# Gate transposition moved behind a projection, a key norm root moved ahead of two silus, mask products added ahead of waits, and a feed-forward loop in another order

## The reference

```python
# layer 0, mixer: a delta rule over the 37 tokens, 16 heads of 16
states = scan(rotate(state) + (x @ cond_in_W))            # 128 wide
deltas = rmsnorm(states) @ delta_W                        # q, k, v and gate parts
q, k, v = silu(causal_conv4(x @ ctrl_W + ctrl_b + deltas))
q, k = l2norm(q), l2norm(k)
S = g*S;  S = S + k (x) (beta * (v - k S));  o = q S      # 37 steps per head
x = x + (rmsnorm(o) * silu(gate)) @ out_proj_W.T
# layer 0, feed-forward: quantized, 1024 hidden
y = silu(conv3(bit_linear(act_quant(layernorm(x)), w1)));  x = x + bit_linear(act_quant(y), w2)
# layer 1: softmax attention with 16 heads, then a mixture of 32 experts
# (8 of 32 by a grouped router, and shared experts), weights streamed from HBM
```

## Time and profile before

| what | value |
|---|---|
| median of 3 runs | 898.96 us (898.91 to 900.83) |
| profiled execution | 899.29 us, span 897.6 us |
| PE / PEld busy | 762.5 us (85%) / 562.6 us (63%) |
| DVE / ACT / POOL busy | 614.6 us (68%) / 389.3 us (43%) / 185.9 us (21%) |
| mean granted clock of PE | 0.933 |
| chain that ended last | PE 70%, DVE 18%, ACT 5%, issue 4% |

### The profile page before, as it was taken

One profiled execution on the slowest core, in us unless ns is written; L12 is line 12 of the kernel. 1 busy time (PEld: TensorE's weight loads), 2 busy tenths in 40 slices (PEclk: granted clock), 3 DMA queues, 4 the chain that ended last, 5 costly groups with the idle time before them and its releaser, 6 DMA issues.

```text
span 897.6 us, 19046 instructions
## 1 busy us (share of the span) xinstructions
PE 762.5 (85%) x7314; PEld 562.6 (63%) x7314; DVE 614.6 (68%) x974; ACT 389.3 (43%) x559; POOL 185.9 (21%) x197
## 2 busy tenths in 40 slices
PE   4786956989996966877598996699999999999997
PEld 3554735954543654656278884467777777777775
DVE  5796597658877476788767887757777755555554
ACT  5344653620224232765356983434444423333322
POOL 7000791005989801000300430000000000000000
PEclk9986877999999996987999998889999999999999
DMA  8000000020000000010112001044444312222221
GB/s 304 1 1 2 2 1 3 3 95 0 1 0 1 0 2 0 1 33 6 35 30 59 14 28 36 1 148 147 157 151 151 125 53 79 65 68 62 67 65 54
DMA packets 24070, 46.02 MB, mean 51 GB/s; under 512 B 2605, under 2 KB 10541, under 8 KB 23629
## 3 DMA queue, kind: packets, MB, share of 16 engines
q1 hardware_dynamic: 24013, 45.21, 16.5%
HBM read 41.91 MB, written 1.36 MB: 48 GB/s over the span
## 4 chain that ended last, share of the span: by engine, by line
PE 70%; DVE 18%; ACT 5%; issue 4%; POOL 1%; DMA 1%; SPq 0%; DVEq 0%; ACTq 0%; POOLq 0%
PE psum L1765 11%; PE psum L1766 11%; PE psum L1767 11%; PE psum L1941 6%; PE psum L1951 4%; PE psum L825 4%; PE psum L826 4%; PE psum L827 4%; PE psum L2069 1%; DVE arena L1445 1%; PE psum L1991 1%; PE psum L1922 1%; DVE arena L1638 1%; DVE arena L1310 1%; PE psum L2108 1%
## 5 line engine op out<-in xcount | busy, mean ns | idle before, releaser
L1765 PE MATMUL psum<-xh,arena 128*128 128x296 f16 (+1 forms) x664 | 196.4, 296 | 12.0 <-DVE xl L1318 6.3
L1766 PE MATMUL psum<-xl,arena 128*128 128x296 f16 (+1 forms) x664 | 196.3, 296 | 0.0
L1767 PE MATMUL psum<-xh,arena 128*128 128x296 f16 (+1 forms) x664 | 196.1, 295 | 0.0
L694 DVE TENSOR_TENSOR arena<-arena 128x592 f16<-128x592 f32 x68 | 52.7, 776 | 61.2 <-ACT arena L605 60.9
L600 ACT ACTIVATE arena<-psum 128x592 f32<-128x592 f32 x66 | 43.8, 664 | 115.3 <-PE psum L1767 115.3
L1765 PEld LDWEIGHTS psum<-xh,arena 128*128 (+2 forms) x664 | 66.2, 100 | 35.6 <-issue 9.4
L749 DVE TENSOR_TENSOR arena<-psum,arena 128x592 f32<-128x592 f32 x64 | 49.6, 775 | 50.9 <-PE psum L1767 50.2
L825 PE MATMUL psum<-arena 128*128 128x296 f16 x272 | 79.7, 293 | 4.6 <-DVE arena L694 3.8
L826 PE MATMUL psum<-arena 128*128 128x296 f16 x272 | 79.7, 293 | 0.0
L605 ACT ACTIVATE arena<-arena 128x592 f16<-128x592 f32 x66 | 46.0, 697 | 77.6 <-DVE arena L688 74.8
L827 PE MATMUL psum<-arena 128*128 128x296 f16 x272 | 79.6, 293 | 0.0
(11 more groups left out here) (317 smaller groups left out, 1583.1 us busy)
## 6 DMA issues: line engine op xcount, KB each, us to landing
arena<-comb SPq DMA_DIRECT2D x62, 296.0 KB, 3.3
arena<-in_wmoe SPq DMA_DIRECT2D x34, 384.0 KB, 3.0
arena<-in_xt SPq DMA_DIRECT2D x4, 864.0 KB, 9.5
arena<-in_w SPq DMA_DIRECT2D x2, 1024.0 KB, 6.6
arena<-arena SPq DMA_DIRECT2D x6, 187.0 KB
arena<-in_ctrl SPq DMA_DIRECT2D x1, 1056.0 KB, 9.1
out<-arena SPq DMA_DIRECT2D x2, 512.0 KB, 3.1
arena<-in_wlin SPq DMA_DIRECT2D x1, 768.0 KB, 4.4
```

Source lines behind the costliest of these rows:

```text
L694: dve.tensor_tensor(al[:, s_], t1, ah[:, s_], ALU.subtract).then_inc(ev["al"], 1)
L1765: pe.matmul(dst, wh, mh, start=start, stop=False)
L1766: pe.matmul(dst, wh, ml, start=False, stop=False)
L1767: return pe.matmul(dst, wl, mh, start=False, stop=stop)
```

## The change

Five things are changed.

1. `dbT` stands behind all four qkv(1, q), on PE, on ACT (its sigmoid) and in the plan of the banks.
2. ACT takes the root of `n2` right behind the evacuation of qkv(5), ahead of silu(4) and silu(5); DVE takes the reciprocal before the two `low_v` steps, and the second of them stands behind the first quarter of `n2r`.
3. `keep_clock(ps, n)` puts n products of the mask with the identity (128 x 296, bf16) into a bank that the next result will overwrite, ahead of a wait of PE. The numbers are in the table `KEEP`; the rec entry is used five times (four layer norms and `cr`), split three times, tok twice, the others once: 5 x 16 + 3 x 12 + 2 x 12 + 18 + 12 + 20 + 12 + 12 + 14 + 36 + 32 + 30 + 24 = 350 products. Where `fill` stood behind a wait it now stands ahead of it.
4. `AT` is made by a plain f32 product with the identity in place of a transposition, and only of the columns from s0 on.
5. In the feed-forward loop `fab` has 4 slots, the absolute values of a pair are taken one iteration later and in the order odd, even, the running maximum stands between the evacuation of `f1` and the convolution (LARGEST is its order), and the last four maxima are taken at the end. Row 0 is scaled on DVE straight out of PSUM, in three pieces, before ACT copies the factors to SBUF (`mx2_read`).

```diff
--- before.py
+++ after.py
@@ -122,9 +122,9 @@
         for q in range(NCH):
-            if m == 1 and q == 2:
-                add(("dbT",), "act")
             add(("qkv", m, q), "act")
+        if m == 1:
+            add(("dbT",), "act")
     add(("n2",), "act")
@@ -200,9 +200,12 @@
 ROUNDED = (0, 2, 4, 6)
+LARGEST = (1, 0, 3, 2, 5, 4, 7, 6)
 HIGH_AT = [7, 9, 11, 13]
...
 FILLERS = 4
+KEEP = {"rec": 16, "mx1": 18, "tok": 12, "xq": 12, "mx2": 20, "hq": 12, "split": 12, "combine": 12, "op": 14, "csq": 36,
+        "qkrec": 32, "km": 30, "on": 24}
 VT = (B + 2) // 3
@@ -428,7 +431,7 @@
         ft = carve(5120, 2, T)
-        fab = carve(33964, 2, T)
+        fab = carve(33964, 4, T)
@@ -852,6 +855,8 @@
                 if hf == 0:
+                    after(pe, ("ln4", "m", 1))
+                    keep_clock(banks[GATE_UP], KEEP["split"])
                     pe.wait_ge(ev["ln4_xl"], 2)
@@ -1113,7 +1118,7 @@
                                        bias=sm("dbb", rows=slice(0, 32))).then_inc(ev["dbh"], 1)
-            for q in range(2):
+            for q in range(NCH):
                 projected(1, q)
@@ -1126,16 +1131,16 @@
                     return
+                act.activation(vh[:, m - 4], post[:, m], ACT.Copy).then_inc(ev["vh"], 1)
+
+            for m in range(1, 6):
+                if m >= 2:
+                    act.wait_ge(ev["conv"], m - 1)
+                for q in range(NCH if m == 1 else 0, NCH):
+                    projected(m, q)
                 if m == 5:
...
                     act.activation(nrm, bank(("n2",))[:, 0:CH], ACT.Sqrt, bias=eps[:, 1:2]).then_inc(emptied["act"], 1)
-                act.activation(vh[:, m - 4], post[:, m], ACT.Copy).then_inc(ev["vh"], 1)
-
-            for m in range(1, 6):
-                if m >= 2:
-                    act.wait_ge(ev["conv"], m - 1)
-                for q in range(2 if m == 1 else 0, NCH):
-                    projected(m, q)
                 through_silu(m - 1)
@@ -1211,17 +1216,29 @@
                         full(act, (name, kind, n))
+                        if (name, kind) == ("mx2", "r"):
+                            act.wait_ge(ev["mx2_read"], n + 1)
                         act.activation(dst[:, 512 * n:512 * n + w], bank((name, kind, n))[:, 0:w], ACT.Copy).then_inc(emptied["act"], 1)
...
             act.activation(warm[:, 1:2], eps[:, 0:1], ACT.Silu)
+            def magnitudes(f):
+                act.wait_ge(ev["sil"], f // 2 + 1)
+                after(act, ("fc", f + 1, NCH - 1))
+                for x in (f + 1, f):
+                    if f >= 4:
+                        act.wait_ge(ev["am2"], LARGEST.index(x - 4) + 1)
+                    act.activation(fab[:, x % 4], sil[:, x], ACT.Abs).then_inc(ev["fabs"], 1)
+
             for f in range(0, FC, 2):
...
                                         bias=sm("fcb", f)).then_inc(ev["fy"], 1)
+                if f:
+                    magnitudes(f - 2)
                 for q in range(NCH):
@@ -1229,19 +1246,17 @@
                 act.activation(sil[:, f], fy, ACT.Silu).then_inc(ev["sil"], 1)
-                act.wait_ge(ev["sil"], f // 2 + 1)
-                after(act, ("fc", f + 1, NCH - 1))
-                for x in (f, f + 1):
-                    if f:
-                        act.wait_ge(ev["am2"], x - 1)
-                    act.activation(fab[:, x % 2], sil[:, x], ACT.Abs).then_inc(ev["fabs"], 1)
+            magnitudes(FC - 2)
             act.wait_ge(ev["l_wqkv"], 16)
...
             for i, f in enumerate(ROUNDED):
-                act.wait_ge(ev["scaled"], i + 1)
+                if i:
+                    act.wait_ge(ev["scaled"], i)
+                else:
+                    act.wait_ge(ev["mx2_read"], 3)
                 link(act.activation(sil[:, f], sil[:, f], ACT.Identity, bias=eps[:, 2:3]))
@@ -1453,12 +1468,13 @@
                         low_db(3)
-            for m in range(2):
+            def low_v(m):
                 dve.wait_ge(ev["vh"], m + 1)
                 dve.tensor_tensor(vl[:, m], post[:, 4 + m], vh[:, m], ALU.subtract).then_inc(ev["vl"], 1)
-                if m == 0:
-                    after(dve, ("n2",))
-                    dve.reciprocal(nrm, nrm).then_inc(ev["qkrec"], 1)
+
+            after(dve, ("n2",))
+            dve.reciprocal(nrm, nrm).then_inc(ev["qkrec"], 1)
+            low_v(0)
@@ -1474,6 +1490,8 @@
                     low_qk(m - 1)
+                else:
+                    low_v(1)
             low_qk(3)
@@ -1632,11 +1650,12 @@
-            def largest(f):
-
-                dve.wait_ge(ev["fabs"], f + 1)
-                dve.tensor_tensor(am, fab[:, 0] if f == 0 else am, fab[:, f % 2], ALU.max).then_inc(ev["am2"], 1)
-                dve.wait_ge(ev["am2"], f + 1)
+            def largest(i):
+                dve.wait_ge(ev["fabs"], i + 1)
+                if i:
+                    dve.wait_ge(ev["am2"], i)
+                now = fab[:, LARGEST[i] % 4]
+                dve.tensor_tensor(am, am if i else now, now, ALU.max).then_inc(ev["am2"], 1)
@@ -1649,24 +1668,30 @@
                                                  wsum[:, 2:3], mxb[:, cols(q)], ALU.mult, ALU.mult).then_inc(emptied["dve"], 1)
+                if f >= 4:
+                    largest(f - 4)
+                    largest(f - 3)
                 dve.wait_ge(ev["fy"], f // 2 + 1)
...
                                                   y[:, :, 0:S - 1], ALU.mult, ALU.add).then_inc(ev["fconv"], 1)
-                if f:
-                    largest(f - 2)
-                    largest(f - 1)
-            largest(FC - 2)
-            largest(FC - 1)
+            for i in range(FC - 4, FC):
+                largest(i)
             token_max("mx2")
...
             dve.tensor_tensor(gwl, gwr, gwh, ALU.subtract).then_inc(ev["gwl"], 1)
+            for n in range(3):
+                t = slice(512 * n, min(512 * n + 512, T))
+                full(dve, ("mx2", "r", n))
+                dve.tensor_tensor(sil[:, 0, t], sil[:, 0, t], bank(("mx2", "r", n))[:, 0:t.stop - t.start], ALU.mult).then_inc(
+                    ev["mx2_read"], 1)
+            dve.wait_ge(ev["mx2_read"], 3)
             after(dve, ("mx2", "r", 2))
-            for f in range(FC):
+            for f in range(1, FC):
                 if f in ROUNDED:
@@ -1766,6 +1791,11 @@
+            def keep_clock(ps, n):
+                for _ in range(n):
+                    pe.matmul(ps[:, 0:8 * S], identb, causalb.unsqueeze(1).to_broadcast([128, 8, S]), start=True,
+                              stop=True)
+
             def norm(name, source, lead=None):
@@ -1785,6 +1815,9 @@
                 ins.then_inc(filled[who((name, "v"))], 1)
+                if name == "ln1":
+                    pe.wait_ge(ev["masks"], 1)
+                keep_clock(fill((name, "r", 0)), KEEP["rec"])
                 pe.wait_ge(ev[name + "_rec"], 1)
@@ -1807,8 +1840,10 @@
             def condition(i, q):
+                ps = fill(("p", i, q))[:, 0:CH]
+                if (i, q) == (0, 0):
+                    keep_clock(ps, KEEP["split"])
                 pe.wait_ge(ev["ln1_xl"], q + 1)
-                ps = fill(("p", i, q))[:, 0:CH]
                 for k in range(2):
@@ -1850,9 +1885,12 @@
             for q in range(NCH):
+                if q == 2:
+                    keep_clock(fill(("cr", 0)), KEEP["csq"])
                 pe.wait_ge(ev["csq"], q // 2 + 1)
...
             ins.then_inc(filled[who(("cv",))], 1)
+            keep_clock(fill(("cr", 0)), KEEP["rec"])
             pe.wait_ge(ev["crec"], 1)
@@ -1867,17 +1905,17 @@
                 for q in range(NCH):
-                    if m == 1 and q == 2:
-                        after(pe, ("db", NCH - 1))
-                        ps = fill(("dbT",))
-                        for t in range(S):
-                            for hg in range(HG):
-                                dst = ps[32 * hg:32 * hg + 32, 8 * t:8 * t + 8]
-                                pick = identh[0:32, 0:32].rearrange("p (i x) -> p i x", i=2)[:, :, 4 * hg:4 * hg + 4]
-                                pe.matmul(dst, seq(dbh)[:, :, t], pick, start=True, stop=False)
-                                ins = pe.matmul(dst, seq(dbl)[:, :, t], pick, start=False, stop=True)
-                        ins.then_inc(filled[who(("dbT",))], 1)
                     projection(m, q)
+                if m == 1:
+                    after(pe, ("db", NCH - 1))
+                    ps = fill(("dbT",))
...
+                    ins.then_inc(filled[who(("dbT",))], 1)
@@ -1887,6 +1925,7 @@
             ins.then_inc(filled[who(("n2",))], 1)
+            keep_clock(fill(("n2r", 0, 0)), KEEP["qkrec"])
             pe.wait_ge(ev["qkrec"], 1)
@@ -1907,6 +1946,8 @@
                     _, j, c, n_ = key
+                    if (j, c, n_) == (0, 0, 0):
+                        keep_clock(ps, KEEP["km"])
                     pe.wait_ge(ev["km"], 2 * j + c + 1)
@@ -1919,7 +1960,10 @@
                     for x in range(ns):
```

(39 more changed lines are left out.)

16 lines of the change are left out of this document (12 added, 4 removed).

## The result

| | median | lowest to highest | profiled execution |
|---|---|---|---|
| before | 899.89 us (4 runs) | 898.91 to 901.34 | 899.29 us, clock 0.933 |
| after | 957.28 us (4 runs) | 944.18 to 963.64 | 963.64 us, clock 0.898 |

The ratio is 1.0529, with an interval of [1.0457, 1.0601]; it compares the two runs of 944.18 and 951.06 alone, because those of 963.50 and 963.64 count as slow ones by their time, while the median of all four is 6.4% above that of before. The forecast was 901.0 with a range from 885 to 912. The runs after are spread over 19.5 us, which the kernel before never showed.

A forecast was written before the change was run, and what follows sets the result against it. The prediction saw two kinds of time to win, PE's waits at seams between stages and its half-clock work, with the A stage PE-bound. Gains against +22.9 for AT, +1.4 and +0.8 summed to +1.75: 901.0 us, range 885 to 912.

The forecast's parts named there:

- I add 1.4 for the last groups, of 7 and 1 times: A stage: allowance on top of +22.9 for AT's loads; a lost clock, up to 5 us more, was the upper end.
- The fourth rival: A stage loses its clock in AT as in dbT, 0.50 for 10 to 20 us: +5 to +10, 908 us; chance 0.07.
- The third convolution: Front: earlier dbT and warmer products let it begin at 97.4 in place of 103.75, 6.3 us won, bounds 5.0 and 7.2.
- what was taken for the root: Key norm: reciprocal ends 3.0 us sooner, against a second table load of 1.28; 1.8 us won, bounds 0 and 3.0.
- the warm A stage: Start of the A stage: part of 3.89 us at half clock saved by warmth, 1.3 us won, at most 1.9.
- The gate transposition's move: Front: the changed order of dbT by itself, counted as 1.0 us won.
- Output norm and ln2 to `xq`: Output norm net 0.4 us won; ln2 and mx1, with warmer broadcast and sums, 1.6 won, bounds 0 and 2.5.
- The loop, mx2 and ln3: Feed-forward loop 4.3 us won by moving absolute values and maxima, mx2 1.9, third layer norm 1.3.
- ln4 and combine with what follows: Fourth layer norm 2.75 us won by warmer products; combine and the products behind it 1.7, bounds 0 and 4.4.
- The first (the seams give more): Won terms at their upper bounds, clock held at nearly every seam: 891 us, or 895 two thirds there; chance 0.22.
- the second (cheap `AT`): A stage: plain products pipeline at the transposition's pace or better, +9.6 and below; 887 or 876 us; chance 0.13.
- The third (the products don't hold the clock): At the seams, added products run out before waits end: 918 us, or 910 with half the warmth; chance 0.2.

The follow-up runs named there:

- the cut version alone: The kernel before with only AT changed, to plain f32 products of the columns from s0 on; 959.45 us, ratio 1.0649.
- the moves alone: The changed kernel with AT transposed again and all KEEP numbers at 0; 895.43 to 897.35 us (three runs) and 919.88 to 922.05 (four).
- the transposed version: The changed kernel with AT made by the 148 transpositions again; 905.24 us, ratio 1.004.
- the experiment: The changed kernel with AT transposed, no added products at the third layer norm, and feed-forward loop and row 0 as before; 885.98 us.

## Why the prediction was wrong

**The step that failed** is the sentence "I add 1.4 for the last groups, of 7 and 1 times", with its bound "up to 5 us more". The clock cost 35.2 there: the stage grew by 58.1, of which 22.9 was forecast for the loads. The pace of a load was right to 2%, 0.112 for 0.11. The fourth rival named the mechanism (the f32 pairs at 0.50, as in `dbT`) and had a chance of 0.07 and 5 to 10 us; it took the loss for a spell that ends by itself. In the trace it ended only behind the stage (at 0.50 from 162.5 to 244 us), and in the cut version alone it did the same (88.0 us). The earlier trace rows showed PE at 0.50 while it was busy, and showed it for a stretch of 8 columns a product; the step should have priced the whole stage at half clock as its bound. From the prediction's own numbers the upper bound was not 5 but some 56 us: 23.8 of A products (33.4 less 9.6) and 32.5 of `AT`, each taking twice as long. The prediction's own sign, some 62 us from the first A product to the end of `AT`, came out at 97.5.

**The second step that failed** was not in the sum at all: every stage not touched was taken over at its time of before. The attention lost 23.4 us in the profiled execution. With 23.4 here, 35.2 there, and the forecast's +1.75 less its 1.4, the sum would be 899.3 + 0.35 + 58.6 = 958.2. The 5.4 that are missing to the profiled 963.6 are gains that came out smaller than forecast (below). What brings the second loss on stays open: the runs show that it comes with the added products alone (78.1 us for the stage) as well as with the moves alone (in 4 of 7 runs), and that 17 products in its pauses prevent it but for one short fall.

**The terms one by one.** The third convolution began at 98.08, forecast 97.4 (before 103.75): 5.7 of 6.3 won. From the chain of waits of the changed kernel:

```profile
98.08 0.85 DVE arena L1454
...
117.16 1.37 DVE arena L1460
118.54 1.91 DVE arena L1476
120.45 1.01 DVE arena L1473
...
121.62 1.57 DVE arena L1488 x4
```

The reciprocal (L1476) now follows the last convolution (L1460) at once, as forecast, and the root's load is off the chain. It began 8.8 us earlier than before, 5.7 of these from the front, so 3.1 for the root. But `AT` began only 7.5 earlier (8.1 in the transposed version): what was taken for the root (1.8) and the warm A stage (1.3) came to 1.8 to 2.4 behind the 5.7, and not 3.1. The gate transposition's move, put at about 1, is nothing that can be measured.

Output norm and ln2 to `xq`: 1.4 with the change, forecast 2.0. The loop, mx2 and ln3: 7.5 forecast, 5.9 measured. Of these the loop itself gave 4.0 against the kernel before (30.9 us from the first to the last `f1`, then 27.0) and 5.0 in the experiment, forecast 4.3; mx2 and ln3 gave 2.0, forecast 3.2. ln4 and combine with what follows: 2.2, forecast 4.45. In sum 17.1 won, forecast 22.55 (23.35 less 0.8). The sizes were some 30% too high in sum, and no group was wrong in sign.

**The rivals.** The first (the seams give more) and the second (cheap `AT`) did not happen. The third (the products don't hold the clock) did not: before the attention, they gained 10.0 us by themselves. It had the right sign for a wrong reason. The fourth happened, at three and a half times its upper price of 10 us.

## What to carry to other kernels

Cutting the moving columns of products that are bound by their weight loads saves nothing and can cost PE's clock: here 30.6 us between 74 columns and the needed ones, with the same loads. Price a change of PE's instructions twice, at full clock and with the whole stage at half clock, and look at how many columns its products move and not only at how long PE is busy. A stage that keeps its clock in some runs and loses it in others, as the attention did here, is a risk for every change ahead of it. So put cheap products in its own pauses first (17 of them were worth 20 us here) and compare single runs, not only medians.

## What the runs showed of the hardware

- A stage in which PE is busy in full can stay at 0.50 for as long as it lasts: 76 us in the A stage, 63 us in the attention. Within these stretches PE had no pause to explain it. Ahead of the fall the attention had pauses (PE busy for 9.11 of 12.10 us), the A stage had none (14.50 of 14.50).
- Plain f32 loads of 128 columns come every 0.112 us at full clock and every 0.213 at half clock, a transposition's loads of the same operand every 0.066 at full clock. So the transposition is one load in 0.066 us where the plain product is two in 0.224.
- The same program can fall into either of two times 23 us or more apart, run by run, on one core: 895 and 920, or 884 and 907.
